# Second mix's weights loaded amid the first layer's routed experts and turned at their end; routed weights requested at a scatter

## The reference, cut to what matters

```python
# layer 0, experts: 16 routed, the 4 best for each row, hidden width 256
routed = sum over e: combine[:, e] * (gelu(x @ re_w1[e] + re_b1[e]) @ re_w2[e] + re_b2[e])
x = x + routed + shared
# layer 1, mix: the weights stand with rows and columns swapped
xn  = layernorm(x)
qkv = xn @ Wqkv.T                  # Wqkv is 1536 x 512
y   = (relu(q) (relu(k)^T v) * temperature / clip(relu(q) . ksum, 100)) @ Wproj.T + bproj
x = x + graph_attention(xn) + y
# layer 1, experts: 16 routed, the 2 best for each row, hidden width 384
```

## Time and profile before

| | |
|---|---|
| device time, median of 3 runs (lowest, highest) | 2369.17 us (2367.21, 2369.88) |
| the profiled execution: device time | 2370.24 us |
| its span, first to last instruction | 2368.2 us |
| busy in the span: PE, DVE, ACT, POOL | 92%, 42%, 21%, 12% |
| mean granted clock of TensorE | 0.971 of full speed |
| routed stage of layer 0 | about 833 to 1123 us |
| layer norm | 1123 to 1132.6 us |
| second mix | from 1132.6 us |
| routed stage of layer 1 | about 2102 us to the end |

### The profile page before, as it was taken

The page is one execution under the profiler, slowest core; times in us unless marked ns, Lnnn a source line. Parts: engine busy times, 40 slices in busy tenths (PEclk is TensorE's granted clock), DMA queues, the critical chain, the costliest instruction groups (busy, mean ns, idle before and its releaser), DMA issues. The chain is left out here.

```text
span 2368.2 us, 26639 instructions
## 1 busy us (share of the span) xinstructions
PE 2173.5 (92%) x7344; PEld 1249.5 (53%) x7345; DVE 1003.9 (42%) x2731; ACT 508.1 (21%) x903; POOL 286.6 (12%) x317
## 2 busy tenths in 40 slices
PE   6998889999998988884999989999999999989997
PEld 3444444445455454442544468864478854535554
DVE  7966778302015522112124465511255413725543
ACT  2112221110103022222210144311153212201111
POOL 1200000000000044443210000000000010013333
PEclk9999999999999999997999999999989999999998
DMA  4003000000003257677200000010000001248774
GB/s 125 1 0 117 1 1 18 1 18 0 0 1 126 67 130 175 148 171 165 67 1 4 23 36 1 1 62 0 8 28 1 1 5 57 84 156 243 234 238 97
DMA packets 77201, 154.57 MB, mean 65 GB/s; under 512 B 10217, under 2 KB 21524, under 8 KB 77116
## 3 DMA queue, kind: packets, MB, share of 16 engines
q1 hardware_dynamic: 59452, 113.06, 14.5%
q0 software_dynamic: 17664, 40.43, 8.6%
HBM read 119.50 MB, written 36.18 MB: 66 GB/s over the span
## 5 line engine op out<-in xcount | busy, mean ns | idle before, releaser
L1933 PE MATMUL bank<-arena 125*125 125x257 f32 x1600 | 355.8, 383 | 4.7 <-DVE arena L1852 4.7
L1933 PEld LDWEIGHTS bank<-arena 125*125 125x125 f32 x1600 | 302.2, 189 | 60.5 <-DVE arena L1852 6.3
L2182 PE MATMUL bank<-arena 128*128 x832 | 260.3, 448 | 12.4 <-issue 6.6
L990 PE MATMUL bank<-arena 125*128 125x500 f32 (+1 forms) x720 | 253.5, 513 | 3.1 <-ACT arena L1019 2.3
L481 PE MATMUL bank<-arena 128*125 128x512 f32 x480 | 212.6, 592 | 2.1 <-ACT arena L558 1.0
L2182 PEld LDWEIGHTS bank<-arena 128*128 128x128 f32 x832 | 153.7, 195 | 111.1 <-issue 61.5
L1727 PE MATMUL bank<-arena 128*125 128x512 f32 x480 | 207.8, 592 | 1.0 <-PEq L408 1.0
L990 PEld LDWEIGHTS bank<-arena 125*128 125x128 f32 x720 | 135.5, 189 | 121.1 <-issue 109.7
L2202 PE MATMUL bank<-arena 128*128 x360 | 178.7, 627 | 7.8 <-ACT arena L2259 7.7
L2307 DVE TENSOR_TENSOR arena<-bank,arena 128x384 f32<-128x384 f32 (+1 forms) x104 | 51.6, 497 | 264.6 <-PE bank L2182 248.5
L1911 ACT ACTIVATE arena<-arena 125x625 f32<-125x625 f32 x160 | 134.5, 900 | 102.4 <-DVE arena L1852 102.2
(11 more groups left out here) (332 smaller groups left out, 2259.7 us busy)
## 6 DMA issues: line engine op xcount, KB each, us to landing
arena<-in_L_ffn_expert_w SPq DMA_DIRECT2D x16, 1536.0 KB
arena<-in_L_ffn_re_w SPq DMA_DIRECT2D x32, 512.0 KB
arena<-in_L_ffn_expert_w SPq DMA_DIRECT2D x16, 768.0 KB
arena<-in_L_mix_Wqkv SPq DMA_DIRECT2D x6, 1024.0 KB, 16.3
arena<-in_L_gnn_W SPq DMA_DIRECT2D x3, 2048.0 KB, 8.4
arena<-in_L_ffn_expert_b SPq DMA_DIRECT2D x16, 384.0 KB
token_rows<-arena SPq DMA_DIRECT2D x2, 2500.0 KB
arena<-in_L_gnn_W SPq DMA_DIRECT2D x3, 1024.0 KB, 5.5
```

What stands on the lines that cost most here:

```text
L990: last = pe.matmul(st.bank[4 + n % 4][:, 0:cn], h[s][:, f * P:(f + 1) * P], st.counts[:, s, c0:c0 + cn], start=(s == 0), stop=(s == NT - 1))
L1933: return pe.matmul(st.bank[n % OUTS][0:TS, 0:ONCOL], prob[:, u % 2, s, j * TS:(j + 1) * TS], st.slots[:, head + 1, s, :], start=(s == 0), ...
L2182: last = pe.matmul(st.bank[UP[b][h]][:, 0:WP], xt[b][:, k, :], rt.ring[:, bass.ds(r, 1), k * W + h * WP:k * W + (h + 1) * WP].rearrange("p ...
```

## The change

1. Raw weights of the second mix. Their four 1 MB loads are issued by SP inside the first routed stage, right behind the load of the experts 7 (k), 9 (v), 11 (q) and 13 (output). After PE's last tile of the stage the twelve rows of k, v and q are turned (48 transposes, two PSUM banks in turn) and placed by ACT; `fetch_root` comes after that. In `stage_mix` the eight turns at the head and the four of q in the loop are gone; the four of the output weights stay, in rounds 0 to 3. Places in SBUF are assigned by hand so that both regions are free in the routed stage.
2. In layer 0 SP's wait ahead of an expert's load is on `add_begun` and no more on `down_ready`. The number waited for is the same, so the load of expert e is asked for when the scatter of the first tile of expert e-2 begins.
3. POOL's row lists are two buffers with two copies, in both routed stages. The list for the gather of the next tile is copied ahead of need (`know_get`), so a gather waits for no copy made just before it; for that POOL waits, between gather g and scatter g, until gather g-1 has landed. The list for the scatter (`know_add`) is copied once scatter g-2 has landed, as before, but no more after a wait for a gather.

```diff
-    def load(sp):
-        for j in "kvqo":
+    def load(sp, parts="kvqo"):
+        for j in parts:
...
-                if i < FIRST:
-                    bank = st.bank[i % 4]
...
-                elif relu:
-                    pe.wait_ge(w_placed, FIRST)
...
-            if relu:
-                for i in range(FIRST):
-                    turn_raw(i)
-            else:
+            if not relu:
                 st.counts_bounds = []
...
-                if relu and t < len(raws) - FIRST:
-                    turn_raw(FIRST + t)
+                if relu and t < len(raws):
+                    turn_raw(t)
...
+    RAW = [1, 3]
+    MIX_AT = {7: "k", 9: "v", 11: "q", 13: "o"}
...
                 if e >= R:
-                    sp.wait_ge(down_ready, sp.value_load(rt.done_by[0:1, e - R:e - R + 1], min_val=1, max_val=TILES + 1))
+                    sp.wait_ge(down_ready if SW else add_begun,
+                               sp.value_load(rt.done_by[0:1, e - R:e - R + 1], min_val=1, max_val=TILES + 1))
                 load_expert(sp, rt, kind, ins, e)
+                if mw is not None and e in MIX_AT:
+                    mw.load(sp, MIX_AT[e])
...
-                load(sp)
...
             def gather(g, b):
                 pool.wait_ge(rows_used, g + 3)
-                pool.wait_ge(row_copied, g + 2)
+                pool.wait_ge(get_copied, g + 1)
...
             def add_rows(g, b):
+                pool.wait_ge(row_copied, g + 2)
                 pool.wait_ge(y_made, g + 3)
...
-                pool.wait_ge(rows_loaded[b], i * 16 + (48 - 16 * b))
                 pool.wait_ge(landed[b], i * 16 + (16 - 16 * b))
-                know_row(b, rt.row_of[:, bass.ds(g + AHEAD, 1), :].rearrange("p a w -> p (a w)"))
+                know_add(g, b)
                 gather(g, b)
+                if not last:
+                    pool.wait_ge(rows_loaded[1 - b], i * 16 + 48)
+                    know_get(g + 1, 1 - b)
                 for odd in range(2):
                     pool.wait_ge(landed[odd], earlier[odd])
                 add_rows(g, b)
...
+            if mw is not None:
+                for i, r in enumerate(mw.turns):
+                    if i % KT == 0:
+                        pe.wait_ge(mw.loaded["kvq"[i // KT]], 16)
+                    if i >= 2:
+                        pe.wait_ge(w_placed, i - 1)
+                    for k in range(KT):
+                        last = pe.transpose(st.bank[RAW[i % 2]][:, k * P:(k + 1) * P], mw.raw[:, r, k * P:(k + 1) * P], st.ident)
+                    last.then_inc(raw_turned, 1)
...
+            if mw is not None:
+                for i, r in enumerate(mw.turns):
+                    act.wait_ge(raw_turned, i + 1)
+                    act.copy(mw.w3[:, :, r * P:(r + 1) * P],
+                             st.bank[RAW[i % 2]].rearrange("p (k n) -> p k n", k=KT)).then_inc(w_placed, 1)
                 fetch_root(act, st)
```

More of the change, by code:

```diff
@@ L358, in _, with mix_weights @@
                          st.bank[t % 4][:, 0:KT * TS].rearrange("p (k n) -> p k n", k=KT)).then_inc(placed, 1)
-def mix_weights(nc, ar, wqkv, wout, turned_in):
+def mix_weights(nc, ar, wqkv, wout, turned_in, w3=None, raw=None):
     mw = State()
-    mw.w3 = ar.take(KT * 3 * D).rearrange("p (k n) -> p k n", k=KT)
+    mw.w3 = (ar.take(KT * 3 * D) if w3 is None else w3).rearrange("p (k n) -> p k n", k=KT)
     mw.wo = ar.take(KT * D).rearrange("p (k n) -> p k n", k=KT)
-    mw.raw = ar.take(4 * KT * D).rearrange("p (r n) -> p r n", n=D) if turned_in else None
+    mw.raw = raw.rearrange("p (r n) -> p r n", n=D) if turned_in else None
+    mw.turns = [r for j in (1, 2, 0) for r in range(j * KT, (j + 1) * KT)]
     mw.loaded = {j: nc.alloc_semaphore(name=f"mix_{j}_loaded{int(turned_in)}") for j in "kvqo"}
-    def load(sp):
-        for j in "kvqo":
+    def load(sp, parts="kvqo"):
+        for j in parts:
             c = "qkvo".index(j)
@@ L445, in _ @@
                 pool.tensor_tensor(st.res3[:, t, :], st.res3[:, t, :], brow, ALU.add).then_inc(res_biased, 1)
-        raws = [r for j in (1, 2, 0, 3) for r in range(j * KT, (j + 1) * KT)]
+        raws = range(3 * KT, 4 * KT)
         @block.tensor
@@ L471, in product @@
                     pe.wait_ge(ready[before], i + 1)
-                elif relu:
-                    pe.wait_ge(w_placed, FIRST)
-                if relu:
-                    if what == "q" and t == 0:
-                        pe.wait_ge(w_placed, 3 * KT)
-                elif t == 0:
+                if not relu and t == 0:
                     pe.wait_ge(mw.loaded[what], 16)
@@ L554, in place_raw @@
                 act.wait_ge(raw_turned, i + 1)
[L555 to L558, removed]
+                act.copy(wo[:, :, i * P:(i + 1) * P], st.bank[TURN + i % 2].rearrange("p (k n) -> p k n", k=KT)).then_inc(w_placed, 1)
             def exp(n):
@@ L583, in _ @@
                 act.copy(vals[:, t % 2, :], st.bank[(2 * t + 1) % 4][0:TS, :]).then_inc(ready["v"], 1)
-                if relu and t < len(raws) - FIRST:
-                    place_raw(FIRST + t)
+                if relu and t < len(raws):
+                    place_raw(t)
             if not relu:
@@ L1096, in front_inputs, with stage_experts @@
     return fi
-def stage_experts(nc, st, ar, kind, ins, kept, fi, out=None, load=None):
+def stage_experts(nc, st, ar, kind, ins, kept, fi, out=None, mw=None, free=None):
     total = NE + kind.shared
@@ L1134, in stage_experts @@
     stage_front(nc, st, Arena(ar.whole, ar.at, ar.end - kind.early * SLOT), kind, ins, rt, fi)
-    stage_routed(nc, st, SplitArena(ar.whole, [(DYN, DYN + KT * NODES + NT * D), (ar.at, ar.end - RING_EXPERTS * SLOT)]),
-                 kind, ins, rt, out, load)
+    stage_routed(nc, st, SplitArena(ar.whole, free or [(DYN, DYN + KT * NODES + NT * D), (ar.at, ar.end - RING_EXPERTS * SLOT)]),
+                 kind, ins, rt, out, mw)
 def stage_front(nc, st, ar, kind, ins, rt, fi):
@@ L2024, in _, with stage_routed @@
                 row_moments(dve, st, (t,), summed)
-def stage_routed(nc, st, ar, kind, ins, rt, out, load):
+def stage_routed(nc, st, ar, kind, ins, rt, out, mw):
     F, W, SW = kind.blocks, kind.w1_cols, kind.swiglu
@@ L2044, in stage_routed @@
     weight = ar.take(TILES)
-    own_row = [ar.take(2).bitcast(I32) for _ in range(2)]
+    get_row, add_row = ([ar.take(1).bitcast(I32) for _ in range(2)] for _ in range(2))
     if SW:
@@ L2142, in _ @@
             pool.wait_ge(rt.sums_set, 16 * NT)
+            know_get(0, 0)
             for g in range(2):
-                know_row(g, rt.row_of[:, g + AHEAD, :])
+                know_add(g, g)
+                pool.wait_ge(rows_loaded[g], 32)
                 gather(g, g)
+                if g:
+                    pool.wait_ge(rows_loaded[0], 48)
+                know_get(g + 1, 1 - g)
                 if g:
@@ L2153, in _ @@
                     tile(i, i * 2 + (2 - b), b)
-            tile(more, more * 2 + 1, 1)
+            tile(more, more * 2 + 1, 1, last=True)
             for b in range(2):
```

38 lines of the change are left out of this document (21 added, 17 removed).

## The result

The changed kernel takes 2358.90 us (median of 7 runs, 2358.14 to 2361.76) against 2367.84 us for the kernel before (7 runs beside them). The ratio is 0.9962, interval 0.9951 to 0.9973: 8.9 us faster, half of the 17.7 us that were forecast. The profiled execution has a span of 2357.0 us, 11.2 less than before. I split that span at five marks that both traces have: the first scatter of expert 1, the read of the sums (SP, L123), the moments of the second half, the first product of the mix, and a point late in its loop.

A forecast was written before the change was run, and what follows sets the result against it. The first routed stage was taken as bound by scatter, landing, scatter, its long link the landing beside weight loads. Terms -6.6 - 1.3 - 11.9 + 2.1 + 0 = -17.7 us gave 2351.5 us, range 2337 to 2367.

The forecast's parts named there:

- The bound: First routed stage: chain of scatter, landing, scatter; long link is the landing beside weights, 10.0 us against 5.07 alone.
- Head, loop, sums, turns: Mix head and loop -6.6 us; read of the sums -1.3 us; twelve turns after the stage's last tile hidden, 0.
- Load at a scatter: Routed stage, experts without raw weights: later request gives period 15.5 us; seven experts gain 11.9 us, expert 13 loses 2.1.
- T+8.2, T+10.3 and T+15.5: Counted from an expert's first scatter T: its landing seen, the third scatter, and the period's end at 15.5 us.
- and, as if they were of this length, 1 and 2: Routed stage: experts 1 and 2 counted among the seven that gain 1.7 us each from the later request.
- The raw loads: Routed stage, experts 5, 7, 9, 11 with 1 MB more each: period 17.2 us, what they take now, so 0.
- They flow from T+10 on, over the last scatter's landing: Routed stage: when raw loads flow, T being the expert's first scatter; period between 15.5 (hidden) and 20.5 us.
- The lists: POOL's split row lists, both routed stages: about 0.6 us per copy-held gather goes, other limits take its place: 0.
- the fourth rival: New wait in `tile` for the earlier gather delays the third scatter; periods 17.3 and 22.2, 2386 us; chance 0.08.
- The first (the loads find room): Routed stage: engines only 70% busy, periods 13.9 and 15.9 us, 35.7 us faster, 2333.5 us; chance 0.18.
- The second, a smaller effect of the shift: Routed stage: third scatter delayed about 1.5 us more, periods 17.0 and 17.7, 3.7 us gain, 2365.5 us; chance 0.14.
- The third, turns between queues: Routed stage: SP's and POOL's requests share every engine; periods 15.5 and 20.5, 4.5 us faster, 2364.7 us; chance 0.10.

The follow-up runs named there:

- c4: Kernel before with changes 2 and 3, without change 1 (no raw loads in the stage): 2358.55 us, ratio 0.9960.
- d2: Changed kernel with raw loads k and v asked for at expert 14's first scatter, q and output at expert 15's: 2357.21 us, ratio 0.9956.
- d4: Changed kernel with the raw load of experts 5, 7, 9, 11 asked for when PE has brought down that expert's last tile: 2353.20 us, ratio 0.9934.
- d1: Changed kernel with all four raw loads asked for at the routed stage's start, ahead of expert 3's load: 2352.89 us, ratio 0.9944.
- e1: Changed kernel with raw loads at the stage's start and layer 0's second weights one scatter later: 2345.86 us, ratio 0.9903.
- e2: e1, but POOL waits for gather g-1 and copies the next gather's list after scatter g, not ahead of it: 2334.62 us, ratio 0.9850.
- e3: e1 with change 3 undone (one list copy, made when the gather two before has landed): 2334.51 us, ratio 0.9861.
- c1: Kernel before with change 1 alone; SP asks at down_ready and POOL keeps its one list copy: 2364.77 us, ratio 0.9987.
- c3: Kernel before with change 3 alone (two list buffers, new wait for the gather before): 2366.14 us, ratio 0.9990.
- e4: Changed kernel with change 3 alone undone: 2359.03 us, ratio 0.9961.
- d3: Changed kernel with the second weights of each layer 0 expert asked for one scatter later than the first: 2350.49 us, ratio 0.9934.

## Why the prediction was right or wrong

**The bound (right).** Landing beside weights was the link: c2, which moves the request and nothing else, takes 16.0 us per expert and not 17.2, and the distance from last to next first scatter falls to 5.6 us.

**Head, loop, sums, turns (right).** -6.8 for -6.6, -1.1 for -1.3, and the turns hidden. The 0.3 us beyond the eight turns are the layer norm's: six of its placements ran at the quick pace (3.09 us for six) where five did before, for the granted clock left 0.50 one placement earlier: between 1124 and 1125 us, with the layer norm's products from 1119.93, and before between 1129.5 and 1130.5, with the products from 1124.51.

**Load at a scatter (right in size, wrong in reach).** 15.83 us for 15.5, and copy, third scatter and landing within 0.3 us of T+8.2, T+10.3 and T+15.5. The step that failed is "and, as if they were of this length, 1 and 2". Their rows in the trace before would have shown 15.70 us for three tiles and 20.49 for four, so there was little to gain, and nothing came: 3.4 of the missing 5.7 us in the stage. The same mean of 17.2 hid that the five plain experts had taken 17.66 us and the four others 16.59.

**The raw loads (the term that was mis-sized).** Forecast 17.2 us, measured 17.91, and their own time before was 16.59: +5.3 us for a forecast of 0. About half of that is the load itself, 17.91 for 17.2, and half is the 17.2 taken for the time before, a mean that is not theirs. "They flow from T+10 on, over the last scatter's landing" is wrong. They lie over the first landing (T+10.7 for T+7.9) and leave the last at 5.56 us. The load was priced at 1.7 us; c4 gives 2.1 us for each, and d2 1.7 to 2.4 without weights beside them. It was the moment of the request that the price left out: d4 gives about 0.3 us, and d1 nothing in these experts and 1.5 us for all four at the start.

**Luck.** The measured time lies inside the forecast's range, but the stage gained 4.1 us where 9.8 were forecast, and 2.5 of the 4.1 are experts 12 and 14, for which 0 was forecast. Expert 12's 1.0 us comes with change 2 (10.6 to 10.9 us in every kernel with it except e1, e2 and e3, 11.8 to 11.9 in those without). Of expert 14's 1.5 us most is this one trace of the kernel before: it has 14.83 us, and c1 and c3, which leave the request alone, have 13.66 and 13.92.

**The lists (right for this kernel).** The forecast was 0, and c3 and e4 show no difference. What the change can cost is the fourth rival's wait, below.

**Rivals.** The first (the loads find room) was wrong in its size, but right that room exists: d4 and, but for 1.5 us, d1 use it. The second, a smaller effect of the shift, isn't what happened: it had 17.0 us for a plain expert. The third, turns between queues, is nearest in time, 4.5 us faster where 8.9 were measured and 17.7 forecast, but not in its periods: it had 20.5 us for an expert with a raw load, the forecast 17.2, and 17.91 was measured. The Trainium skill's rule behind it (DMA: Bandwidth & Descriptors, Queues, rings and completion order) agrees with the trace as far as a scatter slows down when a load is asked for beside it, 2 to 3 us for one megabyte. It gives no price for the moment: the same megabyte asked for 4.4 us later slowed the third scatter's landing by 0.4 us (d4), and asked for 1.1 us ahead of a last scatter it left that landing as it was (c1). The fourth's mechanism, the wait for gather g-1, costs nothing in the changed kernel and 11 us in e1: it decides once the landings before it get short.

**Open.** Why a load under the third scatter (d4), or behind 1.2 MB just ahead of it (c1), costs so much less than one under the first wasn't taken apart further; the first scatter also shares the engines with a gather and the second scatter, but no run separates them. c1's median lies 4.2 us above its profiled execution, where the changed kernel's is its own profiled execution, and no run explains that.

## What to carry to other kernels

A mean over periods hides what an edit will meet: read each period that the edit touches, above all those that a forecast would only copy. A load that is off the critical path still has a price, and it depends on which landing is open when its bytes flow; move it by one step of the loop before giving up on it. A wait that costs nothing today may be the next link when the one ahead of it is shortened, so after each gain look at what the same instruction waits for now.

## What the runs showed of the hardware that was not expected

A scattering, accumulating DMA of 256 KB had landed 5.1 us after its start with no load beside it. It was seen landed after 5.7 us with 0.6 MB of weights asked for at the same moment (d3), after 7.9 with 1.2 MB and after 10.7 with 2.2 MB (the changed kernel's two experts above). These three also have a gather and the next scatter beside them, which the first has not. With the 4 MB asked for at the stage's start the engines moved 385 GB/s over 6 us, gathers included, and the first scatter came 1.5 us later, counted from POOL's first list copy.
